# Last pair of row tiles worked tile by tile, and second products in two PSUM banks, in a gated attention and feed-forward kernel

## What is computed

```
h  = silu(bitlinear(layernorm(x), w1, b1))        # 512 -> 2048
h  = gelu(h)
h  = layer_norm(h) * ln_g + ln_b                  # over the 2048 columns
y  = h / rms(h), quantised to integers with one step per row
out = x + tanh(g_ffn) * (y @ w2.T + b2)           # 2048 -> 512
```

## Time and profile before

| | us |
|---|---|
| median of 3 runs | 1796.25 |
| lowest, highest | 1794.05, 1799.43 |
| the profiled execution | 1802.99 |
| its span, first to last instruction | 1801.2 |
| DVE busy | 1642.1 (91%) |
| PE busy | 1537.8 (85%) |
| ACT busy | 1392.2 (77%) |
| POOL busy | 1317.3 (73%) |
| mean granted TensorE clock | 0.959 of full speed |

### The profile page before, as it was taken

How to read it: one execution, slowest core, us unless ns; L and a number is a source line. 1 busy time by engine, 2 the same in 40 slices (tenths; PEclk the granted TensorE clock), 3 DMA queues, 4 the chain that set the end, 5 groups by cost and what they waited for, 6 DMA issues and landing times.

```text
span 1801.2 us, 34644 instructions
## 1 busy us (share of the span) xinstructions
PE 1537.8 (85%) x13190; PEld 753.6 (42%) x13207; DVE 1642.1 (91%) x2209; ACT 1392.2 (77%) x1351; POOL 1317.3 (73%) x1293
## 2 busy tenths in 40 slices
PE   7799967898888889888898988888888887789985
PEld 4344422444444444444444444444444443333331
DVE  7779868999999999999999999999999997489894
ACT  4468767888898888789888888987887887677781
POOL 0156655889989888888988888898988898254531
PEclk9889986999999999999999999999999998899997
DMA  6769986989958999895899988689897877132313
GB/s 218 243 210 344 349 303 122 171 176 172 172 111 147 166 171 178 157 170 109 148 181 167 185 169 151 120 140 164 148 159 136 151 133 147 39 77 53 88 43 75
DMA packets 725640, 286.55 MB, mean 159 GB/s; under 512 B 676121, under 2 KB 680793, under 8 KB 724194
## 3 DMA queue, kind: packets, MB, share of 16 engines
q1 hardware_dynamic: 724098, 281.40, 75.0%
q0 software_dynamic: 704, 1.62, 0.3%
q10 hardware_dynamic: 672, 1.31, 0.2%
HBM read 76.59 MB, written 39.88 MB: 65 GB/s over the span
## 4 chain that ended last, share of the span: by engine, by line
DVE 35%; POOL 22%; PE 14%; issue 11%; ACT 2%; DMA 1%; POOLq 0%; DVEq 0%; SPq 0%; ACTq 0%
DVE att_scaled L1611 32%; POOL att_probsT L1374 18%; PE att_scores L1171 3%; PE att_ps_o L1187 3%; PE att_scores L1111 2%; POOL att_low_row L1364 2%; PE att_scores L1131 2%; POOL att_bias_row L1367 1%; DMA att_pairsT<-att_pairs 1%; PE att_scores L1172 1%; DVE att_v_largest L1580 1%; ACT att_pairs L1247 1%; PE att_scores L1073 1%; DVE att_scaled L1545 1%; DVE att_scaled L1542 1%
## 5 line engine op out<-in xcount | busy, mean ns | idle before, releaser
L1611 DVE TENSOR_SCALAR_CACHE_REDUCE att_scaled<-att_scores,layer_nsq 128x1536 f32<-128x1536 f32 (+1 forms) x768 | 1202.7, 1640 | 24.5 <-PE att_scores L1131 15.9
L1247 ACT ACTIVATE att_pairs<-att_scaled,att_bias_row 128x4096 uint8<-128x4096 f32 x256 | 950.4, 3713 | 146.9 <-DMA att_pairsT<-att_pairs 101.6
L1374 POOL CAST att_probsT<-att_pairsT 128x2048 bf16<-128x2048 uint8 x512 | 953.6, 1891 | 113.7 <-DMA att_pairsT<-att_pairs 100.3
L1131 PE MATMUL att_scores<-first_head_area 96*128 96x512 bf16 x1024 | 299.2, 397 | 96.5 <-DVE att_scaled L1611 79.9
L1131 PE MATMUL att_scores<-att_head_area 96*128 96x512 bf16 x1024 | 287.5, 383 | 67.2 <-DVE att_scaled L1611 64.0
L1092 PEld LDWEIGHTS att_ps_o<-att_v_head,att_probsT 128*128 128x128 bf16 x8192 | 242.9, 96 | 67.7 <-POOL att_probsT L1374 3.8
L1092 PE MATMUL att_ps_o<-att_v_head,att_probsT 128*128 128x32 bf16 x8192 | 245.2, 176 | 4.8 <-DMA att_v_head<-layer_w2T 2.9
L1131 PEld LDWEIGHTS att_scores<-first_head_area 96*128 96x128 bf16 x1024 | 81.8, 99 | 258.2 <-DVE att_scaled L1611 173.3
L1131 PEld LDWEIGHTS att_scores<-att_head_area 96*128 96x128 bf16 x1024 | 79.6, 97 | 215.2 <-DVE att_scaled L1611 152.7
L1073 PE MATMUL att_scores<-att_head_area 96*128 96x512 bf16 x621 | 168.4, 380 | 0.0
L1073 PE MATMUL att_scores<-first_head_area 96*128 96x512 bf16 x570 | 159.2, 389 | 0.0
(11 more groups left out here) (170 smaller groups left out, 1630.0 us busy)
## 6 DMA issues: line engine op xcount, KB each, us to landing
layer_w2T<-ctx_T SPq DMA_DIRECT2D x96, 256.0 KB, 3.9
k_rows<-kv_parts SPq DMA_DIRECT2D x32, 512.0 KB, 4.4
q_w_in<-in_L_ffn_w_dram SPq DMA_DIRECT2D x32, 256.0 KB, 2.8
kv_weights_ctx_in<-in_ctx_dram SPq DMA_DIRECT2D x32, 256.0 KB, 4.8
kv_weights_w_in<-in_L_ffn_w_dram SPq DMA_DIRECT2D x32, 256.0 KB, 4.9
ctx_T<-kv_inT SPq DMA_DIRECT2D x8, 1024.0 KB, 6.3
q_x_in<-in_x_dram SPq DMA_DIRECT2D x16, 256.0 KB, 3.8
terns<-kv_tern SPq DMA_DIRECT2D x32, 128.0 KB, 4.4
```

Source lines behind the costliest of these rows:

```text
L1131: last = pe.matmul(buffer[:, x:x + 512], q_head[slot][:, at:at + P], k_head[slot][:, STARTS[j] + x:STARTS[j] + x + 512], start=True, stop= ...
L1247: act.activation(pairs[g % R_BUFS][:, :].bitcast(U8).rearrange("p (c two) -> p two c", two=2), scaled[u][:, :].rearrange("p (two c) -> p t ...
L1374: pool.tensor_copy(probsT[g % C_BUFS][:, parity * HALF:(parity + 1) * HALF, :].rearrange("p k q -> p (k q)"), bytes_now.rearrange("p (n tw ...
L1611: dve.tensor_scalar(scaled[u][:, STARTS[j]:STARTS[j] + WIDTHS[j]], scores[(g * NCH + j) % 2][:, 0:WIDTHS[j]], kept["nsq"][:, g:g + 1], Non ...
```

## The change

The last pair is taken out of the pair scheme, in all four engine queues, and products go to two banks from tile 11 on.

- `second_product`: tiles 11, 13 and 15 use the bank `ps_v`, the others `ps_o` as before. Product 11 waits for the last read of the input transposes out of `ps_v` (`out_kept`), not for an output; products from 12 on wait for the output of tile i-2 instead of i-1.
- ACT in round 8: gelu 14, deviation 14, gelu 15, deviation 15, instead of both gelus and then both deviations. `square` of tile 14 gets an explicit wait for both deviations, since they share a scratch tile.
- POOL: `invert_dev_alone` and `invert_rms_alone` work one tile of the last pair, with semaphore counts that go on from the pairs'. `invert_dev_alone(14)` stands between the two means, `invert_dev_alone(15)` behind the second, and the two `add_bias_2` of round 8 stand behind it and ahead of `invert_rms_alone(14)`.
- DVE: the loop ends with round 8. Then a list written out: normalise 14, maximum 14, first pass of row 15, steps and quantising 14, output 12, second pass of row 15, maximum 15, output 13, steps and quantising 15, outputs 14 and 15. `normalise` is split into `centre_row` and `scale_row`, and `step_second` into `step_rows` with a range of tiles.
- SP's queue is unchanged: it transposes 14, then 15, then stores 12 and 13, then 14 and 15.

The diff, cut to its core:

```diff
+        LAST, APART = PAIRS - 1, 2 * PAIRS - 5
+        def out_bank(i):
+            return ps_v if i >= APART and i % 2 else ps_o
...
                 def second_product(i):
...
-                    after(pe, result_ready, i)
-                    pe.matmul(ps_o[:, :], less[:, :], sum_parts, start=True, stop=False)
+                    bank = out_bank(i)
+                    if i == APART:
+                        pe.wait_ge(out_kept, QT)
+                    else:
+                        after(pe, result_ready, i if i < APART else i - 1)
+                    pe.matmul(bank[:, :], less[:, :], sum_parts, start=True, stop=False)
...
                     if i % 2:
                         act.wait_ge(y_sq_ready, i)
+                    elif i == 2 * LAST:
+                        act.wait_ge(dev_ready, QT)
...
+                    if r - 1 == LAST:
+                        for i in fed:
+                            gelu(i)
+                            deviate(i)
+                    else:
...
+                def invert_dev_alone(i):
+                    pool.wait_ge(dev_ready, i + 1)
+                    pool.tensor_scalar(dev_mean[:, i:i + 1], dev[:, i:i + 1], 1.0 / INNER, EPS, ALU.mult, ALU.add).then_inc(dev_mean_ready, 1)
+                    pool.wait_ge(dev_mean_ready, i - LAST + 1)
+                    pool.tensor_tensor(rstd_2[:, i:i + 1], dev_mean[:, i:i + 1], power[:, 0:1], ALU.pow).then_inc(rstd_2_ready, 1)
...
-                    if normed:
+                    if r - 2 == LAST:
+                        for i in normed:
+                            invert_rms_alone(i)
+                    elif normed:
                         invert_rms(r - 2)
                     for i in fed:
                         mean(i)
+                        if r - 1 == LAST:
+                            invert_dev_alone(i)
...
-                for r in range(1, PAIRS + 3):
+                for r in range(1, LAST + 2):
...
+                older, (one, other) = pair_of(LAST - 1), pair_of(LAST)
+                normalise(one)
+                largest_2(one)
+                centre_row(other)
+                step_second_alone(one)
+                quantise_second(one)
+                result(older[0])
+                scale_row(other)
+                largest_2(other)
+                result(older[1])
+                step_second_alone(other)
+                quantise_second(other)
+                result(one)
+                result(other)
```

More of the change, by code:

```diff
@@ L1183, in second_product @@
                     pe.wait_ge(ints_2_turned[i % TURN_BUFS], 16 * (i // TURN_BUFS + 1))
-                    after(pe, result_ready, i)
-                    pe.matmul(ps_o[:, :], less[:, :], sum_parts, start=True, stop=False)
+                    bank = out_bank(i)
[4 more added lines that the diff above has]
+                    pe.matmul(bank[:, :], less[:, :], sum_parts, start=True, stop=False)
                     for k in range(IT):
-                        last = pe.matmul(ps_o[:, :], turned[i % TURN_BUFS][:, k, :], kept["w2T"][:, k, :], start=False, stop=(k == IT - 1))
+                        last = pe.matmul(bank[:, :], turned[i % TURN_BUFS][:, k, :], kept["w2T"][:, k, :], start=False, stop=(k == IT - 1))
                     last.then_inc(out_ready, 1)
@@ L1344, in _ @@
                         keep_heads(UNITS - 2)
[L1345 to L1354, removed]
+                    if r - 1 == LAST:
[3 more added lines that the diff above has]
+                    else:
+                        for i in fed:
+                            gelu(i)
+                        if r == 1:
+                            keep_heads(UNITS - 1)
+                        if fed:
+                            deviate(fed[0])
+                        if mixed:
+                            centre(mixed[1])
+                        if fed:
+                            deviate(fed[1])
                     for i in mixed:
@@ L1483, in _ @@
                         split_inverse(r)
-                    if fed:
+                    if fed and r - 1 != LAST:
                         invert_dev(r - 1)
@@ L1537, in quantise_first, with centre_row @@
                                       ALU.mult, ALU.add).then_inc(upped_1_ready, 1)
-                def normalise(i):
+                def centre_row(i):
                     row = rows[i % ROW_BUFS]
@@ L1542, in normalise, with scale_row @@
                     dve.scalar_tensor_tensor(row, row, mean_neg[:, i:i + 1], ln_g, ALU.add, ALU.mult).then_inc(u_ready, 1)
-                    dve.wait_ge(rstd_2_ready, i // 2 + 1)
+                def scale_row(i):
+                    row = rows[i % ROW_BUFS]
+                    dve.wait_ge(rstd_2_ready, i // 2 + 1 if i < 2 * LAST else i - LAST + 1)
                     dve.wait_ge(u_ready, i + 1)
                     dve.scalar_tensor_tensor(row, row, rstd_2[:, i:i + 1], ln_b, ALU.mult, ALU.add).then_inc(y_ready, 1)
+                def normalise(i):
+                    centre_row(i)
+                    scale_row(i)
                 def largest_2(i):
@@ L1550, in largest_2, with step_rows @@
                                       apply_absolute_value=True).then_inc(y_max_ready, 1)
[L1552 to L1557, removed]
+                def step_rows(first, stop, order, rms_done):
+                    done = PER_2 * order
+                    part = [row_2[:, n, first:stop] for n in range(4)]
+                    dve.wait_ge(rms_ready, rms_done)
+                    dve.wait_ge(y_max_ready, stop)
+                    dve.tensor_tensor(part[0], y_max[:, first:stop], rms[:, first:stop], ALU.mult).then_inc(row_2_math, 1)
                     dve.wait_ge(row_2_math, done + 1)
@@ L1561, in step_second, with step_second_alone @@
                     dve.reciprocal(part[2], part[1]).then_inc(row_2_math, 1)
-                    dve.tensor_scalar(both(step_2, r), part[1], w2_step[:, 0:1], None, ALU.mult).then_inc(row_2_math, 1)
+                    dve.tensor_scalar(step_2[:, first:stop], part[1], w2_step[:, 0:1], None, ALU.mult).then_inc(row_2_math, 1)
                     dve.wait_ge(row_2_math, done + 4)
-                    dve.scalar_tensor_tensor(part[3], part[2], 127.0, both(rms, r), ALU.mult, ALU.mult).then_inc(row_2_math, 1)
+                    dve.scalar_tensor_tensor(part[3], part[2], 127.0, rms[:, first:stop], ALU.mult, ALU.mult).then_inc(row_2_math, 1)
                     dve.wait_ge(row_2_math, done + 5)
+                def step_second(r):
+                    step_rows(2 * r, 2 * r + 2, r, r + 1)
+                def step_second_alone(i):
+                    step_rows(i, i + 1, i - LAST, i - LAST + 1)
                 def quantise_second(i):
```

7 lines of the change are left out of this document (6 added, 1 removed).

## The result

| | us |
|---|---|
| kernel before, median of 4 | 1795.9 (1794.05 to 1799.43) |
| changed kernel, median of 4 | 1785.13 (1784.48 to 1786.96) |
| ratio | 0.9939, 95% interval 0.9922 to 0.9957 |
| span of the profiled execution | 1782.8 (before: 1801.2) |

What follows compares the result with a forecast made beforehand. Bound: a tail latency chain of about 50 us, DVE waiting 21.2 us for second products. Gains of 5.1 and 4.4 us ended the span at 1791.7, 9.5 under 1801.2; 1796.25 − 9.5 = 1786.8 us, range 1781.0 to 1792.5.

Steps and rivals of the forecast that it cites:

- the rival of the free port: Last pair: GpSimd's small instructions get in before DVE's passes, so waits are not paid; gain 12.1 us, 1784.2; chance 0.18.
- Part 1: Second bank for products 11, 13, 15: product 11 follows product 10 at once, removing DVE's wait of 5.87 us.
- Inversion 14: GpSimd, row 14: held until DVE's first pass ends (2.34 us, the upper bound), then 0.2 us, and 0.7 for the power.
- The meeting of first pass, additions and inverse 14: Row 15's first pass on DVE meets GpSimd's bias additions near 1764.65; inverse ready near 1769.0, DVE waits 1 to 2 us.
- Steps 14: DVE, behind the inverse root mean square of row 14: 1.0 us, then quantising 1.25 us, to 1771.25.
- quantising 15: DVE's last quantising, behind the inverse of row 15 at 1777.4: ends with its steps at 1779.65.
- The DMA of row 15: Last transposing DMA, covered before and now on the path: 4.7 us, landing at 1784.4.
- Product 14 at the half clock: TensorE, after 10 us idle: 6.8 us from 1776.0 to 1782.8, still ahead of the landing of row 15.
- Product 15 at the full clock: TensorE, idle only 1.7 us before it, less than 4 us, so full clock: 1784.5 to 1788.4.
- DVE's earlier start on row 14: DVE's first pass of row 14 starts at 1756.86 instead of 1761.92: 5.1 us of the gain.
- the shorter way from there: From row 14 to the end: products no longer queue behind outputs, net of GpSimd waits and uncovered DMA; 4.4 us.
- the late step: Tail: slower DMA (1.4 us), mean 15 caught (2.4) or product 15 at half clock (2.8); 1788.2 to 1789.6; chance 0.14.

Runs made afterwards that it cites:

- bias_late: Changed kernel with the two bias additions of tiles 14 and 15 moved behind DVE's last quantising: tail 53.73 us against 54.84, ratio 0.9946 to the kernel before.
- one DMA more: One additional transposing DMA of row 15 ahead of the real one: tail 59.65 us in the changed kernel (54.84 without), 65.64 in the kernel before (65.81 without).
- spare matmuls ahead of both: Changed kernel with 30 matmuls whose results nobody reads ahead of product 14 and 14 more ahead of product 15: tail 54.90 us against 54.84.
- the repeat: The changed kernel measured once more, nothing altered: tail 54.92 us against 54.84, ratio 0.9943 to the kernel before.
- the split alone: Changed kernel with all second products in one bank again, each waiting for the previous tile's output: tail 62.51 us against 65.81 before, ratio 0.9989.
- the banks: Kernel before with only the two product banks and their new waits, last pair still worked as a pair: tail 59.96 us against 65.81, ratio 0.9954.
- spare products ahead of 14: Changed kernel with 30 matmuls whose results nobody reads ahead of product 14 only: tail 56.52 us against 54.84, ratio 0.9942 to the kernel before.

## Why the prediction was right

The number alone doesn't show it: 1785.13 is 1.7 us below the forecast and 0.9 us above the rival of the free port (1784.2). What shows it are the steps, here with 7.43 us added to the times of the changed kernel:

- Part 1. Product 11 at 1751.08 right behind product 10 and at the full clock, outputs 10 and 11 done at 1755.96 (said: 1756.05), first pass over row 14 at 1756.85 (1756.86), released by ScalarE. Right to 0.1 us.
- Inversion 14 held by DVE's pass: 2.35 us, as the upper bound had it; DVE was first by 0.05 us. The power took 0.55 us and not 0.70, since it works on one element per partition and not two; second pass at 1759.91 (1760.10). The free-port rival is out: it would have had about 0.2 us for the inversion in this place.
- The meeting of first pass, additions and inverse 14 ended at 1768.40 (1769.0). The mechanism was in the main the one forecast: additions hold the pass, the inverse of row 14 comes out only behind it, and DVE waits 0.71 us (said: 1 to 2). The term was a little too large: the additions took 2.50 us and not 4.54, since only the second met a pass. `bias_late` shows what it costs: 1.1 us.
- Steps 14 took 0.88 us, not 1.0; the forecast had the inverse of row 15 end behind output 13, and it ended just ahead of it; quantising 15 ended at 1778.63 (1779.65), 1.0 us early from the sum of these small terms.
- The DMA of row 15: 4.4 us from the end of the quantising to product 15, for 4.8; product 15 at 1783.02 (1784.5). That it is on the path, and was covered before, is shown by the pair with one DMA more: 4.8 us in one kernel, none in the other.
- Product 14 at the half clock 6.4 us (6.8), behind 7.37 us of idle time and not 10, and off the path: shown by the kernel with spare matmuls ahead of both. Product 15 at the full clock behind 1.7 us of idle time: right, and the repeat agrees (1.64 us). The reason given, that 1.7 us is less than the 4 us after which the clock had fallen, was weaker than it looked: the clock fell behind 3.03 us in this same trace (product 12) and behind 2.37 us with the split alone. Nor did the prediction say that the idle time is short because product 14 is slow.
- The end at 1790.2 (1791.7): gain 10.97 for 9.5. All of the 1.5 us is the small terms above and the DMA's landing; none is a mechanism of its own. Of the gain 4.99 us is DVE's earlier start on row 14 (said: 5.1) and 5.98 us the shorter way from there (4.4).
- The prediction put the split alone at about 5.5 us. It gave 3.30, or 4.98 without the fall of the clock in product 15; on top of the banks it brings 5.12 (59.96 to 54.84).
- Of the rivals, the late step appeared in the neighbours of this kernel: product 15 lost 1.7 to 2.3 us to the clock in three of them (split alone, spare products ahead of 14, one DMA more), with TensorE idle for 2.4 to 4.2 us ahead of it, but not in the changed kernel itself, with 1.7 us.

## What to carry to other kernels

At the end of a pipeline each engine's program is a latency chain: follow it event by event from a shared starting point, and measure it from such a point, since that reads tenths of a microsecond where the medians of this 1.8 ms kernel scatter by several microseconds. A second buffer for the consumer's last tiles and a split of the last pair each brought their own part here, but together they took the cover off something else: a DMA's landing, a small instruction behind another engine's pass, and the clock of the next product. Ask of every slow piece that is off the path what it hides before making it faster.

## What the runs showed that was not expected

- Making a product faster made the tail longer, in one profiled execution: with product 14 at 3.9 us instead of 6.4, TensorE was idle 4.16 us, the granted clock fell to 0.50 behind it, and product 15 took 5.31 us for 3.63; the tail grew by 1.68 us.
- An idle time of 2.37 us ahead of product 15 already ended in a fall of the clock, in the middle of the product (1784 to 1785 in the kernel with the split alone), while 2.7 us in the one with the additions late did not. What tells the two apart is left open; in the two traces of the changed kernel the same 3.0 us ahead of product 12 ended once in a fall and once not.
- A transposing DMA of half the row landed 3.1 to 3.2 us behind its issue, the whole one 4.3 us; its issue held SyncE's queue 1.2 to 1.3 us against 1.7 and 2.0 for the whole ones of tiles 14 and 15. Halving this DMA saved about a quarter of its latency, not half.
- GpSimd's power on 128x1 took 0.55 us and on 128x2 0.70.
